# New durations in the list scheduler of a fused attention and mixture-of-experts block

## The reference

```
h = layernorm(x) * (1 + ca) + sa
x = x + ga * attn1(h)          # 16 heads of 8, bias by relative position, softmax
h = layernorm(x) * (1 + cb) + sb
x = x + gb * ffn(h)
# ffn(x):
h = x + attn2(rmsnorm(x))      # 16 heads of 8, rotary, causal mask, softmax
y = h + moe(rmsnorm(h))        # router, best 2 of 8 experts, hidden width 384, gated
```

## Time and profile before

| | us |
|---|---|
| median of 3 runs (1076.97 to 1079.93) | 1079.14 |
| the profiled execution's own time | 1078.02 |
| its span | 1076.2 |
| TensorE busy | 925.0 (86%) |
| VectorE busy | 696.7 (65%) |
| ScalarE busy | 481.0 (45%) |
| GpSimd busy | 201.8 (19%) |

### The profile page before, as it was taken

How to read it: one execution, slowest core, us unless ns; L and a number is a source line. 1 busy time by engine, 2 the same in 40 slices (tenths; PEclk the granted TensorE clock), 3 DMA queues, 4 the chain that set the end, 5 groups by cost and what they waited for, 6 DMA issues and landing times.

```text
span 1076.2 us, 39365 instructions
## 1 busy us (share of the span) xinstructions
PE 925.0 (86%) x16386; PEld 610.7 (57%) x16386; DVE 696.7 (65%) x1464; ACT 481.0 (45%) x814; POOL 201.8 (19%) x244
## 2 busy tenths in 40 slices
PE   4787899998999999899998989999999979888841
PEld 2445465565656556565654656666566757666730
DVE  1564677777686777768678776677686464656623
ACT  1343455545555554555554445555455434333310
POOL 1340021202111220211112020201110010155225
PEclk9887899999999999999999999999999999999985
DMA  7389100000000000000000000000001011134313
GB/s 223 140 316 386 54 9 16 17 7 18 7 23 8 17 18 7 17 8 22 7 18 17 23 26 13 27 18 22 28 24 35 26 40 37 48 109 135 93 47 91
DMA packets 50299, 59.08 MB, mean 55 GB/s; under 512 B 6672, under 2 KB 37392, under 8 KB 49744
## 3 DMA queue, kind: packets, MB, share of 16 engines
q1 hardware_dynamic: 36272, 28.24, 8.5%
q10 hardware_dynamic: 9760, 19.92, 5.0%
q0 software_dynamic: 4096, 8.40, 2.7%
HBM read 22.92 MB, written 33.62 MB: 53 GB/s over the span
## 4 chain that ended last, share of the span: by engine, by line
PE 74%; DVE 11%; issue 6%; ACT 4%; DMA 2%; POOL 2%; SPq 1%; POOLq 0%; DVEq 0%; ACTq 0%
PE ps L792 9%; DVE row_max L1155 6%; PE ps L893 6%; PE ps L648 6%; PE ps L885 5%; PE ps L681 5%; PE ps L659 5%; PE ps L693 5%; PE ps L638 3%; ACT probs L992 3%; PE ps L816 3%; PE ps L887 3%; PE ps L639 3%; PE ps L623 3%; PE ps L629 3%
## 5 line engine op out<-in xcount | busy, mean ns | idle before, releaser
L1155 DVE TENSOR_REDUCE row_max<-ps 128x4 f32<-128x1024 f32 (+1 forms) x256 | 271.8, 1087 | 83.0 <-PE ps L659 50.6
L992 ACT ACTIVATE probs<-ps 128x1024 f32<-128x1024 f32 x128 | 130.5, 1024 | 84.8 <-PE ps L681 82.3
L992 ACT ACTIVATE stage<-ps 128x1024 f32<-128x1024 f32 x96 | 98.1, 1024 | 85.9 <-PE ps L687 85.2
L885 PE MATMUL ps<-xT_t,wgu_hi 128*128 128x128 f16 x480 | 101.7, 225 | 33.5 <-issue 31.2
L648 PE MATMUL ps<-bias_t,ch 64*32 64x512 f16 x2048 | 109.8, 392 | 13.4 <-DVE q_rows L1172 6.2
L1375 POOL TENSOR_TENSOR rstd_n<-var_n,cf 128x2 f32<-128x2 f32 x48 | 34.0, 709 | 453.1 <-DVE var_n L1084 453.1
L1306 DVE SCALAR_TENSOR_TENSOR gate_s<-gate_t,ps 128x256 f32<-128x256 f32 x120 | 50.2, 418 | 79.1 <-ACT gate_t L1042 73.3
L886 PE MATMUL ps<-xT_t,wgu_hi 128*128 128x128 f16 x480 | 99.0, 219 | 0.0
L887 PE MATMUL ps<-xT_t,wgu_lo 128*128 128x128 f16 x480 | 98.9, 219 | 0.0
L1042 ACT ACTIVATE gate_t<-ps 128x256 f32<-128x256 f32 x120 | 46.1, 384 | 107.2 <-PE ps L887 93.3
L792 PE MATMUL ps<-probs,v_pad 128*32 128x256 f32 x1024 | 83.6, 398 | 4.6 <-ACT probs L992 3.8
(11 more groups left out here) (171 smaller groups left out, 1810.3 us busy)
## 6 DMA issues: line engine op xcount, KB each, us to landing
slot_rows<-gate_s ACTq DMA_DIRECT2D x1, 12032.0 KB, 35.6
slot_rows<-gate_s ACTq DMA_DIRECT2D x1, 7424.0 KB, 31.3
x_t<-slot_rows SPq DMA_DIRECT2D x80, 64.0 KB, 1.9
slot_rows<-eo_t SPq DMA_DIRECT2D x80, 64.0 KB
xT<-in_x SPq DMA_DIRECT2D x16, 128.0 KB, 2.0
kept<-resid SPq DMA_DIRECT2D x16, 128.0 KB, 1.8
resid_b<-kept SPq DMA_DIRECT2D x16, 128.0 KB, 2.5
out_dram<-outT SPq DMA_DIRECT2D x16, 128.0 KB, 2.0
```

The source lines that it names most:

```text
L885: eng.matmul(dst, wgu_hi[:, w, block], x_hi, start=True, stop=False)
L992: eng.activation(probs[a][:, 2 * (k % 2):2 * (k % 2) + 2, :], ps[:, lo:lo + 2, :], ACT.Exp).then_inc(z["exp"], 1)
L1155: ins = eng.tensor_reduce(row_max[a][:, qt, 4 * g:4 * g + 4].rearrange("p (r j) -> p r j", r=2), of_heads, AX.X, ALU.max)
```

## The change

The table of durations and overlaps gets other numbers. A step of VectorE or ScalarE now lets the engine's next one start before it has ended (GAP below zero); s, e and c steps get shorter, gu steps longer, and a change of tile kind costs 0.095 for 0.08. Nothing else in the program is edited.

```
-GAP = {"pe": 0.0, "act": 0.03, "dve": 0.03, "pool": 0.05, "sp": 0.1}
+GAP = {"pe": 0.0, "act": -0.09, "dve": -0.08, "pool": 0.05, "sp": 0.1}
...
-            last = self.op((job, i, "s%d" % t), "pe", 0.46, [last], CORE, mode=1)
+            last = self.op((job, i, "s%d" % t), "pe", 0.44 if a == 1 or len(gs) > 1 else 0.33, [last], CORE, mode=1)
...
-                self.op(key + ("pe",), "pe", 0.66, before + xt, banks)
+                self.op(key + ("pe",), "pe", 1.0 if c else 2.2, before + xt, banks)
```

More of the change, by code:

```diff
@@ L161, in core @@
         for t, (qt, gs) in enumerate(SCORES[a]):
-            last = self.op((job, i, "s%d" % t), "pe", 0.46, [last], CORE, mode=1)
-            self.op((job, i, "m%d" % t), "dve", 1.2 * len(gs) - 0.1 * (len(gs) - 1) if len(gs) == 1 else 1.4, [last], (), "mine")
+            last = self.op((job, i, "s%d" % t), "pe", 0.44 if a == 1 or len(gs) > 1 else 0.33, [last], CORE, mode=1)
+            self.op((job, i, "m%d" % t), "dve", 1.15 if len(gs) == 1 else 1.2, [last], (), "mine")
         last = self.op((job, i, "mx"), "dve", 0.6, [(job, i, "m%d" % t)], ("max_rows",))
@@ L169, in core @@
             if sid[0] == "e":
-                pe = self.op((job, i, sid), "pe", 0.46, [pe], CORE, mode=1)
+                pe = self.op((job, i, sid), "pe", 0.44 if a == 1 or len(PAIRS[a][k][1]) > 1 or not PAIRS[a][k][0] else 0.33, [pe], CORE, mode=1)
                 self.op((job, i, "x%d" % k), "act", 1.05, [pe] + ([(job, i, "c%d" % (k - 2))] if k > 1 else [])
@@ L173, in core @@
             else:
-                pe = self.op((job, i, sid), "pe", 0.57, [pe, (job, i, "x%d" % k)] + ([(job, i, "vz")] if not k else []),
+                pe = self.op((job, i, sid), "pe", 0.45, [pe, (job, i, "x%d" % k)] + ([(job, i, "vz")] if not k else []),
                              (X,) if not k else (), mode=2)
@@ L301, in run @@
                 if eng == "pe" and m != mode:
-                    t, mode = t + 0.08, m
+                    t, mode = t + 0.095, m
                 clock[eng] = t + us + GAP[eng]
```

## The result

The changed kernel takes 1092.72 us (median of 6 runs, 1090.55 to 1096.20), the kernel before 1078.06 on the same chip. The ratio is 1.0137 (95% interval 1.0118 to 1.0157): 15 us slower, where 1099 was forecast. The profiled execution took 1092.39, its span is 1090.6 us. The total came out near the forecast by luck: two of its terms were wrong by 19 and by 16 us, with opposite signs.

The account below looks back on a forecast made before the run. TensorE, busy 86%, was taken as the bound: 44.2 us of matmuls and tile changes plus 2.8 of waits per middle item. 31 + 1 - 10 - 2 = +20 on 1078.0 gave 1098, as median 1099 us; range 1074 to 1114.

Parts of the forecast that it names:

- The burst: c2's s1 to s5 back to back at VectorE's pace: 6.6 to 6.9 us to the e step, TensorE losing 3.9.
- The middle: Items 2 to 9: waits grow from 2.8 to 4.8 us, plus 2.0 per item, 3.9 with the clock's fall; +31 us.
- The clock: Behind each burst, for most items, about 6 us at half clock, ending 1.9 us later; bounds 0 and 3.0.
- The start: Load wait gone, item 1's first e step at 81 to 87 us, item 0's burst lost: -10 us, bounds -16 and -4.
- The load's wait: At the start, the 4.96 us wait for item 3's load goes, since the load should have landed by then.
- The rule of exclusion: GpSimd and fast-mode VectorE instructions exclude each other; k_head could slip in before the split, putting the start at -16 us.
- Items 10 to 15: Item 10 +1 us for one more s step in its burst; items 11 to 15, with the moe steps, -2.
- The tail: Gathers, accumulation and output at the end keep their order: 0 us.
- The signs: Middle period 50 to 51 us, three or four L659 waits of about 0.6, lowered clock, first e step before 90.
- The first: Rival: the middle's bursts come without the fall of the clock, +5 us in all, 1084 us; chance 0.18.
- The faster case: Rival: start wins 16 us, moe stretch 6 to 8, middle loses only 6; about 1062, milder 1070; chance 0.12.

Follow-up runs that it names:

- fill: Changed kernel with the score matmuls of s2 to s5 of c2 run twice in items 2 to 10, same values written again: 1080.05 us, 1.0019.
- no_gu: Changed kernel with the old duration of the gu steps (0.66), all other numbers new: 1084.61 us, 1.0048.
- tail_short: Changed kernel with gu long only in the moe part of the first ten items, 0.66 in the part around the final steps: 1080.99 us, 1.0020.
- m_only: Kernel before with only the new m step durations (1.15 for 1.2, and 1.2 for 1.4 with two groups): 1064.86 us, 0.9874.
- no_gap: Changed kernel with the old overlaps GAP (0.03 for VectorE and ScalarE), all other numbers new: 1073.26 us, 0.9955.

## Why the prediction came out as it did

The total was 1099 us for 1092.7, and the direction right. Step by step:

- **The burst** is as described: five s steps and the e step in VectorE's pace, 6.8 us from s0 to the e step (6.6 to 6.9 forecast), in items 2 to 10.
- **The middle, +31 us: mis-sized, it is +12.4.** The step that failed is the 2.0 us per item at full clock; it measures 0.3 (47.3 us where the clock stays, 47.0 before; 2.2 us in eight items in fill). I set losses that I had worked out from start to start (3.9 + 0.6 + 0.3) against the 2.8 us of idle time that the view of waits shows before. That view has the changed kernel at 2.7 as well. It counts from a matmul's end, and the end lies behind the point where the next one could start. Take instead the time from a matmul's start to the next one's start, less what the same pair takes in these traces where nothing waits. On that measure the six waits of before come to about 3.5 us. In a period of the changed kernel at full clock the four waits of the burst come to 3.3 and the two others to 0.5, together 3.8. So the burst costs almost nothing at full clock: it replaces waits of nearly the same sum elsewhere in the period.
- **The clock, +1.9 us for each fall: right in size** (49.15 - 47.3 = 1.85). It fell in six of eight items and not in all; in no_gu and tail_short it fell in all eight.
- **The start, -10: it is -6.** The load's wait went as forecast and the first m step came at 71.75, but the first e step of item 1 came at 89.94 and not between 81 and 87. Two us of the missing four are k_head: it took 8.85 us and not 7.46, and TensorE's wait for it grew from 2.8 to 4.9. The rest is no property of the order: fill has the same order up to there, the same 8.85 and 4.92, and reached -8.9, with its k_head starting 2 us earlier and the clock at 0.86 from 30 to 90 us where it was 0.80 here. m_only and no_gap reached -10. The rule of exclusion was named, but only as the good end of the range; it struck the other way.
- **Items 10 to 15, -1: about -4**, beside 4 us that only moved into the tail.
- **The tail, 0: wrong, it is +12.** "Keeps its order" was the failed step. I had looked at the gathers and the accumulation and not at how far apart the final steps stand among the moe steps, although the new length of gu acts on just that. The price of the last table line of the diff was never worked out.
- **The signs.** The waits at L659, the load and the first e step under 90 us came as named. The period of 50 to 51 us did not come: it is 48.6 in the mean.
- **The rivals.** The first (no fall of the clock, 1084) described fill, 1080. The faster case asked for less than 1.5 us per middle item and a good start; the middle came to 1.55 and the start to -6, and the tail, which no case held, added 12.

So the forecast was near by luck: +19 too much in the middle stood against 12 to 16 too little in the tail.

## What to carry to other kernels

A list scheduler's table is not improved by making each number truer. Of this change the m steps alone gain 13 to 14 us. The shorter s, e and c steps on top of them cost 5 (1070.3 against 1064.9). The overlaps cost 19 (1092.7 against 1073.3), over half of it by the clock, which the planner does not model. And the longer gu costs 9 to 12 where final steps stand between the gu steps, and gains some 6 where they don't. Test the numbers one by one, and compare two orders start to start, at fixed milestones, never the idle time shown in the one with losses worked out for the other. Where an engine's steps stand back to back behind a slower engine's pace, look at the clock before the waits.

## What the runs showed of the hardware

- Repeating matmuls in the gaps of a burst made the kernel 12.6 us faster. The clock fell behind six of eight bursts in which TensorE idled 0.6 us between steps (behind all eight in two other kernels with these bursts), and behind none when the gaps were filled to 0.4 us.
- Two VectorE steps of 1.0 and 0.35 us took up to 8.85 and 5.58 us beside GpSimd instructions of 2.7 to 6.1 us over SBUF, and 1.51 and 0.35 when these were cut into four.
- The kernel before took 1078 to 1079 us on two chips and 1176 on a third, there with VectorE's reductions standing up to 5.1 us, and ScalarE as well, for a releaser that the trace doesn't show, at the two places read (157 and 361 us) beside GpSimd's indirect DMAs. Only ratios to the kernel before on the same chip can be compared.
